# First expert's first two up-projection tiles done in token halves, and slot parts made with one operation fewer

## The chip, the cores and the metric

The kernel runs on one core of one Trainium2 chip. The metric is the device time of one execution in microseconds (us), read as the median over runs. All engine names below are those of the profile: PE is the matrix engine (PEld its weight loads), DVE the vector engine, ACT the scalar engine, POOL the engine that issues the gathers, SP the engine that issues plain transfers.

## What is computed

One layer: linear attention with a residual and a normalisation over 4096 tokens of 256 numbers, then a feed-forward block in which each of 8 experts picks its own 512 tokens. All values are float32. Cut to what matters here, the second half is

```python
logits = xf @ Wr + br                       # xf: 4096 x 256
Sm = softmax(logits, axis=-1)
G_t, idx_t = jax.lax.top_k(Sm.T, 512)       # each expert takes its 512 best tokens
tokens = xf[idx]                            # 512 rows per expert
mid = silu(einsum('keh,ehf->kef', tokens, W_up[group]) + b_up[group])   # 256 -> 682
out = einsum('kef,efh->keh', mid, W_down) + b_down                      # 682 -> 256
y = zeros_like(xf).at[idx].add(G[..., None] * out)
x = layernorm(x + y)
```

## The kernel before, in words

The program is one straight piece of code per engine; the engines meet only at semaphores, and each engine takes its instructions in the order in which they are written. The attention and the router take the first 172 us. Then the tokens of the experts are chosen, and the eight experts follow each other on PE to the end.

**Choosing tokens.** The router's probabilities lie as 128 partitions (32 token tiles x 4 experts) by 128 tokens. For experts 0 to 3 the threshold is searched in 15 rounds (lines 1075 to 1096), before any expert starts. `choose(0, ...)` (line 1098) then gives every chosen token its place in the expert's list, 1 to 512, and 0 to the others; PE turns that array (L752), and DVE splits place - 1 into the number of a list row (`part_f`, the slot divided by 4) and the column in it (`four_f`, the remainder). This takes five operations, L1128 to L1134: subtract 1 and make whole numbers, shift right, mask, and a cast of each of the two. `spread(e)` (line 1159) compares `part_f` with a constant ramp, `iotas`, and so makes 32 one-hot matrices in bfloat16 (`hot`); `lists(e)` on PE multiplies them with a small payload, which yields the token numbers of expert e (`numbers(e)` writes them to `idx`).

For experts 4 to 7 the threshold search is hidden behind the first two experts. It has ten rounds, and one round is a loop between two engines: `guess(r)` on DVE counts seven candidate thresholds, `count_second(r)` on PE adds the counts up (L757, one small matmul), `settle(r)` on DVE reads the sums (L1154) and fixes the next threshold. DVE's order around the first expert is written out by hand:

```python
numbers(1)
settle(0)      # waits for count_second(0) on PE
gates(0)
guess(1)
spread(2)
settle(1)      # waits for count_second(1) on PE
for e in range(LATE):
    expert(e)  # expert 0 begins with guess(2), settle(2), guess(3), settle(3)
```

**An expert.** POOL gathers the expert's 512 rows in four indirect transfers of 128 rows each (L1481), for expert 0 with one semaphore each. PE turns every row tile (`turn(e)`, L785, two 128x128 transposes a row tile, into banks 2 and 3 of the accumulator memory, one bank for each half of the 256 features). ACT copies both banks into `xgt` (L1378). PE multiplies `xgt` with the up weights in six feature tiles f = 0 to 5 (L798); each tile takes two matmuls of 512 columns, one for each half of the features, and every float32 matmul stands as two records in the trace. ACT applies the activation (L1383). Then follow `lists` and `turn` for later experts, and the down projection (L829), 48 records of 256 columns.

Around expert 0, PE's order before is: `lists(0)`; two 512-column filler matmuls (`warm`, L840, whose result nobody reads); `lists(1)`; `turn(0)` with a 256-column filler between its second and third row tile; `count_second(0)`; another 256-column filler; the six tiles of the up projection, with `count_second(1)` after f = 1, `count_second(2)` after f = 3 and `count_second(3)` after f = 5; then `lists(2)`, `turn(1)` and the down projection. From then on DVE makes rounds 4 to 9 of the search and the one-hot matrices of later experts while PE works.

Of the kernel before, what the change touches and what calls it, by code (L numbers as in the profile page):

```python
# [27 lines left out]
P = 128  # L28
ALU = mybir.AluOpType
# [4 lines left out]
I32 = mybir.dt.int32  # L34
# [3 lines left out]
C = D // P  # L38
# [4 lines left out]
BLK = TB * P  # L43
NT = N // P
NB = NT // TB
HALVES = BLK // 2
E = 8
GS = 2
G = E // GS
F = int(D * 4 * (2.0 / 3.0))  # L50
FT = -(-F // P)
FR = F - (FT - 1) * P
KSEL = N // E
KT = KSEL // P
# [3 lines left out]
EH = E // 2  # L58
# [42 lines left out]
def constants():  # L101
# [8 lines left out]
    c[:, C_BEFORE:C_BEFORE + P] = (p[:, None] % EH == p % EH) & (order[:, None] < order)  # L110
    c[:, C_IOTA:C_IOTA + P] = p
    c[:, C_HEAD8:C_HEAD8 + HH] = p[:, None] // HD == np.arange(HH)
# [20 lines left out]
def build(nc, x, xt, xtq, wqkv, bq, bv, wp, wpn, cols, rows, wr, wup, bup, wdn, cst, steps, out):  # L133
    with ExitStack() as ctx:
        def sb(name, shape, dt=F32):
            return ctx.enter_context(nc.sbuf_tensor(name, shape, dt))

        def sem(name):
            return ctx.enter_context(nc.semaphore(name))
# [100 lines left out]
        slot_i = sb("slot_i", [P, P], I32)  # L240
        part_i = sb("part_i", [P, P], I32)
        part_f = sb("part_f", [P, E, NT], BF16)
# [126 lines left out]
        s_gate = sem("s_gate")  # L369
        s_xtmm = sem("s_xtmm")  # L370
        s_xt = sem("s_xt")
        s_umm = sem("s_umm")
# [219 lines left out]
        def _(pe):  # L592
# [181 lines left out]
            def turn(e):  # L774

                if e:

                    pe.wait_ge(s_gat[e % 2], 16 * KT * (e // 2 + e % 2))
                for k in range(KT):
                    if e == 0:  # L780
                        if k == KT // 2:
                            warm(1, BLK // 2)
                        pe.wait_ge(s_first[k], 16)
                    for c in range(C):
                        mm = pe.transpose(ps[:, 2 + c, k * P:(k + 1) * P], xg[:, e % 2, k, c * P:(c + 1) * P], ident)  # L785
                mm.then_inc(s_xtmm, 1)

            def expert(e):
                last = e == E - 1
                pe.wait_ge(s_xt, C * e + C)  # L790
                if e % GS == 0:
                    pe.wait_ge(s_wup, 16 * (e // GS) + 16)
                for f in range(FT):
                    width = P if f < FT - 1 else FR
# [5 lines left out]
                    mm.then_inc(s_umm, 1)  # L800
                    if e == 0 and f == 1:
                        count_second(1)
                    if e < 2 and f in (3, FT - 1):
# [41 lines left out]
            lists(1)  # L845
            turn(0)
            count_second(0)
            warm(1, BLK // 2)

# [5 lines left out]
        def _(dve):  # L855
# [242 lines left out]
            def choose(h, values, level_):  # L1098
# [26 lines left out]

                done, bank, half = 5 * h, 7 if h else 0, slice(EH * h, EH * (h + 1))
                dve.wait_ge(s_pickmm, h + 1)
                dve.tensor_scalar(slot_i[:], ps[:, bank, CH:CH + P], -1.0, None, ALU.add).then_inc(s_slot, 1)  # L1128
                dve.wait_ge(s_slot, done + 1)
                dve.tensor_scalar(part_i[:], slot_i[:], KT.bit_length() - 1, None, ALU.arith_shift_right).then_inc(s_slot, 1)  # L1130
                dve.tensor_scalar(four_i[:], slot_i[:], KT - 1, None, ALU.bitwise_and).then_inc(s_slot, 1)
                dve.wait_ge(s_slot, done + 3)
                dve.tensor_copy(part_f[:, half, :], part_i[:].rearrange("p (s e) -> p e s", e=EH)).then_inc(s_slot, 1)
                dve.tensor_copy(four_f[:, half, :], four_i[:].rearrange("p (s e) -> p e s", e=EH)).then_inc(s_slot, 1)  # L1134
                dve.wait_ge(s_slot, done + 5)

# [162 lines left out]
        def _(act):  # L1299
# [91 lines left out]
            act.sem_inc(s_mid, 2)  # L1391
            turn(0)
            for e in range(LATE):
# [197 lines left out]
```

## Time and profile before

| what | value |
|---|---|
| median of 3 runs | 435.29 us (434.12 to 436.79) |
| the profiled execution, its own time | 434.87 us |
| its span in the trace | 433.1 us |
| PE busy | 368.4 us (85%) |
| DVE busy | 236.6 us (55%) |
| ACT busy | 147.7 us (34%) |
| POOL busy | 164.8 us (38%) |
| chain that ended last, by engine | PE 61%, DVE 12%, POOL 11%, DMA 5%, issue 5% |
| largest lines of that chain | L829 16%, L798 15% (both PE, the experts) |

The time of an execution is its span and some 1.8 us around it. The chain of work that ended last is followed back from the last instruction, at each step to what released it. "Granted clock" (PEclk) is the rate that TensorE was given, 1.00 for 2.4 GHz and 0.50 for 1.2 GHz. In a row of the timeline the first number is the start in us from the span's start, the second the time taken, and a bracket says how long the engine was idle before the row and what ended the idling. Rows that follow each other with the same shape are merged (x2, x8); where two kinds of rows overlap on one engine, the later starts before the earlier has ended, since the array is pipelined.

### The profile page before, as it was taken

What the parts mean: (1) busy time and instruction counts of PE and PEld (TensorE: products, weight loads), DVE (VectorE), ACT (ScalarE), POOL (GpSimd) and SP (SyncE); (2) the same over time, 40 slices, a digit from 0 to 9 for tenths busy, and PEclk for the clock granted to TensorE, in tenths of its full rate; (3) what the DMA queues carried; (4) which work ended last, traced back from release to release, by engine and by line L of the source; (5) the groups of instructions that cost most, each with busy time, mean ns of one, the idle gap of its engine ahead of it and who ended that gap; (6) DMA issues with size and microseconds to landing.
All of it is one profiled execution on the core that took longest, in us unless ns stands there. A gap on an engine that the chain in (4) does not pass through costs nothing.

```text
span 433.1 us, 5640 instructions
## 1 busy us (share of the span) xinstructions
PE 368.4 (85%) x1651; PEld 244.4 (56%) x1651; DVE 236.6 (55%) x885; ACT 147.7 (34%) x350; POOL 164.8 (38%) x250
## 2 busy tenths in 40 slices
PE   8899999899997980114899999999999999999920
PEld 7788886467775650003447565573856657374610
DVE  0775554787889888878663745513130301059450
ACT  2333323344686884330031220403112030346600
POOL 0310053001567884001703542336344243564853
PEclk9999999999999996555699999999999999999985
DMA  8935444500133554900301452416343262699641
GB/s 252 353 105 190 149 147 145 178 0 2 51 123 116 178 176 143 10 0 2 92 9 51 89 117 81 57 50 113 116 89 51 70 131 53 113 297 375 215 150 48
DMA packets 50046, 50.75 MB, mean 117 GB/s; under 512 B 12169, under 2 KB 43234, under 8 KB 50018
## 3 DMA queue, kind: packets, MB, share of 16 engines
q1 hardware_dynamic: 44066, 40.32, 31.5%
q0 software_dynamic: 5952, 10.10, 11.7%
q8 instruction: 13, 0.21, 0.2%
q14 instruction: 15, 0.12, 0.1%
HBM read 32.97 MB, written 17.43 MB: 116 GB/s over the span
## 4 chain that ended last, share of the span: by engine, by line
PE 61%; DVE 12%; POOL 11%; DMA 5%; issue 5%; SPq 3%; ACT 2%; POOLq 0%; DVEq 0%; ACTq 0%
PE ps L829 16%; PE ps L798 15%; PE ps L633 6%; PE ps L625 6%; PE ps L609 5%; PE ps L770 3%; PE ps L706 3%; POOL rstd L1435 3%; DMA heads<-ysum,idx 2%; DVE qexp L1054 2%; PE ps L719 2%; PE ps L785 1%; DMA heads<-xt 1%; POOL ysum L1488 1%; POOL xg L1481 1%
## 5 line engine op out<-in xcount | busy, mean ns | idle before, releaser
L829 PE MATMUL ps<-wdn_s,ht_all 128*128 128x256 f32 (+1 forms) x384 | 95.4, 394 | 0.0
L798 PE MATMUL ps<-xgt,wup_s 128*128 128x512 f32 (+1 forms) x192 | 87.5, 608 | 0.1
L829 PEld LDWEIGHTS ps<-wdn_s,ht_all 128*128 128x128 f32 (+1 forms) x384 | 67.8, 189 | 24.9 <-issue 18.4
L1383 ACT ACTIVATE ht_all<-ps,bup_s 128x512 f32<-128x512 f32 (+1 forms) x48 | 33.0, 687 | 122.1 <-PE ps L798 122.1
L1481 POOL DMA_INDIRECT xg<-table,idx x32 | 32.3, 1010 | 89.2 <-DVE idx L1181 46.4
L798 PEld LDWEIGHTS ps<-xgt,wup_s 128*128 128x128 f32 (+1 forms) x192 | 33.2, 182 | 47.6 <-issue 47.6
L1488 POOL DMA_INDIRECT ysum<-yb,idx x24 | 40.6, 1693 | 46.6 <-DVE yb L1213 41.1
L1213 DVE TENSOR_SCALAR yb<-ps,gate 128x256 f32<-128x256 f32 x24 | 11.6, 484 | 55.7 <-PE ps L829 55.7
L609 PE MATMUL ps<-wqkv_s,heads 128*128 128x264 f32 x128 | 33.3, 410 | 1.8 <-DMA heads<-xt 1.8
L719 PE MATMUL ps<-wp_s,turned 128*128 128x264 f32 x128 | 33.7, 385 | 0.0
L625 PE MATMUL ps<-h_all,heads 128*128 128x258 f32 (+1 forms) x128 | 30.4, 382 | 0.0
L633 PE MATMUL ps<-ht_all,wqkv_s 128*128 128x512 f32 x64 | 30.2, 594 | 0.0
L609 PEld LDWEIGHTS ps<-wqkv_s,heads 128*128 128x128 f32 x128 | 25.8, 203 | 7.0 <-issue 2.4
L625 PEld LDWEIGHTS ps<-h_all,heads 128*128 128x128 f32 x128 | 24.2, 190 | 4.1 <-DVE heads L903 0.4
L1435 POOL TENSOR_TENSOR rstd<-ve,cs 128x2 f32<-128x2 f32 (+1 forms) x34 | 25.7, 756 | 0.2
L706 PEld LDWEIGHTS ps<-kvk,qt 128*128 128x128 f32 x128 | 18.4, 190 | 11.1 <-issue 6.5
L1307 ACT ACTIVATE heads<-heads 128x512 f32<-128x512 f32 x16 | 10.1, 631 | 39.1 <-DVE heads L895 39.1
L719 PEld LDWEIGHTS ps<-wp_s,turned 128*128 128x128 f32 x128 | 21.8, 190 | 2.3
L1430 POOL TENSOR_TENSOR ve<-mv,cs 128x2 f32<-128x2 f32 (+1 forms) x34 | 8.0, 235 | 37.8 <-ACT z L1331 34.2
L706 PE MATMUL ps<-kvk,qt 128*128 128x136 f32 x128 | 19.7, 285 | 3.0 <-DVE qt L929 2.1
L1338 ACT ACTIVATE x<-us,shift,rstd 128x256 f32<-128x256 f32 x32 | 19.6, 611 | 4.3 <-POOL shift L1440 4.3
L770 PEld LDWEIGHTS ps<-pay,ht_all 128*128 128x128 bf16 x256 | 16.3, 163 | 7.7 <-DVE ht_all L1173 4.8
(193 smaller groups left out, 533.7 us busy)
## 6 DMA issues: line engine op xcount, KB each, us to landing
wdn_s<-wdn SPq DMA_DIRECT2D x8, 640.0 KB
h_all<-x SPq DMA_DIRECT2D x8, 512.0 KB, 5.6
ht_all<-xtq SPq DMA_DIRECT2D x8, 512.0 KB, 3.6
table<-x SPq DMA_DIRECT2D x32, 128.0 KB, 1.7
ysum<-x SPq DMA_DIRECT2D x32, 128.0 KB, 1.8
h_all<-ysum SPq DMA_DIRECT2D x8, 512.0 KB, 8.7
out<-h_all SPq DMA_DIRECT2D x8, 512.0 KB, 5.6
heads<-xt SPq DMA_DIRECT2D x7, 512.0 KB, 4.1
```

The source lines that it names most:

```text
L609: mm = pe.matmul(ps[:, bank + u, 0:D + E], ht_ring[:, j // 2, c, at:at + P], wqkv_s[:, c, D:W_V], start=(c == 0), stop=(c == C - 1))
L625: mm = pe.matmul(ps[:, 2 + c, 0:HC], key[:, back % 4, u, c * P:(c + 1) * P], h_all[:, bass.ds(i * 8 + (2 * back + u), 1), :].rearrange("p ...
L633: mm = pe.matmul(ps[:, m, :], wqkv_s[:, c, m * P:(m + 1) * P], ht_all[:, c, bass.ds(n * BLK, BLK)], start=(c == 0), stop=(c == C - 1))
L706: mm = pe.matmul(ps[:, 2 + t % 2, c * (P + HH):(c + 1) * (P + HH)], qt[:, c, t * P:(t + 1) * P], kvk[:, c, :], start=True, stop=True)
L719: mm = pe.matmul(bank, turned[:, (t - 1) % TB, c, :], wp_s[:, c, :], start=False, stop=(c == C - 1))
L770: mm = pe.matmul(ps[:, 6, 0:2 * KT], hot[:, :, s], pay[:, s].rearrange("p w k -> p (w k)"), start=(s == 0), stop=(s == NT - 1))
L798: mm = pe.matmul(ps[0:width, f % 2, :], wup_s[:, c, f * P:f * P + width], xgt[:, c, :], start=(c == 0), stop=(c == C - 1))
L829: mm = pe.matmul(ps[:, bank, 0:D], mid[0:rows_, f, j * P:(j + 1) * P], wdn_s[0:rows_, f, :], start=(f == 0), stop=(f == FT - 1))
L1383: act.activation(mid[0:width, f, :], ps[0:width, f % 2, :], ACT.Silu, bias=bup_s[0:width, e // GS, f:f + 1]).then_inc(s_mid, 1)
L1435: pool.tensor_tensor(rstd[:, tile, first:last], ve[:, t, first:last], cs[:, C_HALF:C_HALF + last - first], ALU.pow).then_inc(s_rs, 1)
L1481: pool.indirect_dma_start(out=xg[:, e % 2, j, :], out_offset=None, in_=table[:, :], in_offset=bass.IndirectOffsetOnAxis(ap=idx[:, e, j:j + ...
L1488: pool.indirect_dma_start(out=ysum[:, :], out_offset=bass.IndirectOffsetOnAxis(ap=idx[:, e, j:j + 1], axis=0), in_=yb[:, j, :], in_offset= ...
```

## The change

It has two parts.

**The first expert's first two tiles.** `turn(0)` is replaced by `turn_half(0)` and `turn_half(1)`, each for two of the four row tiles; half 0 goes to bank 2 and half 1 to bank 3, with both feature halves in one bank. ACT copies each half by itself (two copies of 2 x 256 elements instead of two of 512). PE's new `first_tiles()` computes f = 0 and f = 1 in four pieces of 256 tokens: f = 0 of half 0, then the turn of half 1, then f = 1 of half 0, then both tiles of half 1. Two 256-column fillers are gone. `count_second(0)`, which stood between the turn and the up projection, now stands after f = 1 of half 0; `count_second(1)` still stands after f = 1. Tiles f = 2 to 5 and everything after them are as before.

**Slot parts.** The shift and its buffer `part_i` are gone. The slot is made as place + 3 in place of place - 1, `part_f` is (place + 3) minus its remainder by 4, read from the accumulator bank again in one combined operation, so it is 4 x (row + 1), and the ramp `iotas` is scaled to match. This runs twice in the program, once for each group of four experts.

```diff
-    c[:, C_IOTA:C_IOTA + P] = p
+    c[:, C_IOTA:C_IOTA + P] = KT * (p + 1)
...
             def turn(e):
 
-                if e:
-
-                    pe.wait_ge(s_gat[e % 2], 16 * KT * (e // 2 + e % 2))
+                pe.wait_ge(s_gat[e % 2], 16 * KT * (e // 2 + e % 2))
                 for k in range(KT):
-                    if e == 0:
-                        if k == KT // 2:
-                            warm(1, BLK // 2)
-                        pe.wait_ge(s_first[k], 16)
                     for c in range(C):
                         mm = pe.transpose(ps[:, 2 + c, k * P:(k + 1) * P], xg[:, e % 2, k, c * P:(c + 1) * P], ident)
                 mm.then_inc(s_xtmm, 1)
 
+            def turn_half(half):
+
+                for k in range(2 * half, 2 * half + 2):
+                    pe.wait_ge(s_first[k], 16)
+                    for c in range(C):
+                        at = c * HALVES + k % 2 * P
+                        mm = pe.transpose(ps[:, 2 + half, at:at + P], xg[:, 0, k, c * P:(c + 1) * P], ident)
+                mm.then_inc(s_xtmm if half else s_halfmm, 1)
+
+            def up_half(f, half):
+
+                at = slice(half * HALVES, (half + 1) * HALVES)
+                for c in range(C):
+                    mm = pe.matmul(ps[:, f, at], wup_s[:, c, f * P:(f + 1) * P], xgt[:, c, at], start=(c == 0), stop=(c == C - 1))
+                return mm
+
+            def first_tiles():
+
+                pe.wait_ge(s_half, 1)
+                pe.wait_ge(s_mid, 1)
+                up_half(0, 0)
+                turn_half(1)
+                pe.wait_ge(s_mid, 2)
+                up_half(1, 0)
+                count_second(0)
+                pe.wait_ge(s_xt, C)
+                for f in range(2):
+                    up_half(f, 1).then_inc(s_umm, 1)
+                count_second(1)
+
...
-                for f in range(FT):
+                for f in range(0 if e else 2, FT):
...
-                    if e == 0 and f == 1:
-                        count_second(1)
...
-            turn(0)
-            count_second(0)
-            warm(1, BLK // 2)
+            turn_half(0)
...
-                done, bank, half = 5 * h, 7 if h else 0, slice(EH * h, EH * (h + 1))
+                done, bank, half = 4 * h, 7 if h else 0, slice(EH * h, EH * (h + 1))
+                turned_ = ps[:, bank, CH:CH + P].rearrange("p (s e) -> p e s", e=EH)
                 dve.wait_ge(s_pickmm, h + 1)
-                dve.tensor_scalar(slot_i[:], ps[:, bank, CH:CH + P], -1.0, None, ALU.add).then_inc(s_slot, 1)
+                dve.tensor_scalar(slot_i[:], ps[:, bank, CH:CH + P], KT - 1.0, None, ALU.add).then_inc(s_slot, 1)
                 dve.wait_ge(s_slot, done + 1)
-                dve.tensor_scalar(part_i[:], slot_i[:], KT.bit_length() - 1, None, ALU.arith_shift_right).then_inc(s_slot, 1)
                 dve.tensor_scalar(four_i[:], slot_i[:], KT - 1, None, ALU.bitwise_and).then_inc(s_slot, 1)
-                dve.wait_ge(s_slot, done + 3)
-                dve.tensor_copy(part_f[:, half, :], part_i[:].rearrange("p (s e) -> p e s", e=EH)).then_inc(s_slot, 1)
-                dve.tensor_copy(four_f[:, half, :], four_i[:].rearrange("p (s e) -> p e s", e=EH)).then_inc(s_slot, 1)
-                dve.wait_ge(s_slot, done + 5)
+                dve.wait_ge(s_slot, done + 2)
+                four = four_i[:].rearrange("p (s e) -> p e s", e=EH)
+                dve.scalar_tensor_tensor(out=part_f[:, half, :], in0=turned_, scalar=KT - 1.0, in1=four,
+                                         op0=ALU.add, op1=ALU.subtract).then_inc(s_slot, 1)
+                dve.tensor_copy(four_f[:, half, :], four).then_inc(s_slot, 1)
+                dve.wait_ge(s_slot, done + 4)
...
             act.sem_inc(s_mid, 2)
-            turn(0)
+            for half in range(2):
+                act.wait_ge(s_xtmm if half else s_halfmm, 1)
+                act.copy(xgt[:, :, half * HALVES:(half + 1) * HALVES],
+                         ps[:, 2 + half, :].rearrange("p (c k) -> p c k", c=C)).then_inc(s_xt if half else s_half, C if half else 1)
```

PE's order from the middle of the first expert's turn to `count_second(1)`, before. L785 is a transpose of a gathered row tile, L840 a filler, L757 a `count_second`, L798 the up projection; the bracket names the semaphores that the instruction waits for (`s_first2` is the third row tile's gather, `s_cnt2` DVE's counts, `s_xt` ACT's copies).

```order
L840 MATMUL ps<-wup_s,cs 128x256
L785 MATMUL ps<-cs,xg 128x128 [waits s_first2]
L785 MATMUL ps<-cs,xg 128x128
L785 MATMUL ps<-cs,xg 128x128 [waits s_first3]
L785 MATMUL ps<-cs,xg 128x128
L757 MATMUL ps<-cnt,same 128x7 [waits s_cnt2]
L840 MATMUL ps<-wup_s,cs 128x256
L798 MATMUL ps<-xgt,wup_s 128x512 [waits s_wup,s_mid,s_xt,s_midone]
L798 MATMUL ps<-xgt,wup_s 128x512
L798 MATMUL ps<-xgt,wup_s 128x512 [waits s_mid]
L798 MATMUL ps<-xgt,wup_s 128x512
L757 MATMUL ps<-cnt,same 128x7 [waits s_cnt2]
```

The same stretch in the changed kernel, from the first piece of the up projection to `count_second(1)`; L789 is `turn_half`, L796 `up_half`, L758 `count_second`.

```order
L796 MATMUL ps<-xgt,wup_s 128x256 [waits s_mid,s_half,s_midone]
L796 MATMUL ps<-xgt,wup_s 128x256
L789 MATMUL ps<-cs,xg 128x128 [waits s_first2]
L789 MATMUL ps<-cs,xg 128x128
L789 MATMUL ps<-cs,xg 128x128 [waits s_first3]
L789 MATMUL ps<-cs,xg 128x128
L796 MATMUL ps<-xgt,wup_s 128x256 [waits s_mid]
L796 MATMUL ps<-xgt,wup_s 128x256
L758 MATMUL ps<-cnt,same 128x7 [waits s_cnt2]
L796 MATMUL ps<-xgt,wup_s 128x256 [waits s_xt]
L796 MATMUL ps<-xgt,wup_s 128x256 x3
L758 MATMUL ps<-cnt,same 128x7 [waits s_cnt2]
```

What moved: the first `count_second` now stands behind two pieces of the up projection and the second half's transposes, and only two pieces of f = 0 and f = 1 stand between it and the next one, where there were a filler and two whole tiles. The fillers are gone.

DVE's order where the slots are split for experts 0 to 3, before, up to the first operation of `spread(0)`.

```order
L1128 TENSOR_SCALAR slot_i<-ps 128x128 [waits s_pickmm]
L1130 TENSOR_SCALAR part_i<-slot_i 128x128 [waits s_slot]
L1131 TENSOR_SCALAR four_i<-slot_i 128x128
L1133 CAST part_f<-part_i 128x128 [waits s_slot]
L1134 CAST four_f<-four_i 128x128
L1164 TENSOR_TENSOR eq<-four_f,cs 128x128 [waits s_slot,s_iotas]
```

The same place in the changed kernel.

```order
L1153 TENSOR_SCALAR slot_i<-ps 128x128 [waits s_pickmm]
L1155 TENSOR_SCALAR four_i<-slot_i 128x128 [waits s_slot]
L1158 SCALAR_TENSOR_TENSOR part_f<-ps,four_i 128x128 [waits s_slot]
L1160 CAST four_f<-four_i 128x128
L1190 TENSOR_TENSOR eq<-four_f,cs 128x128 [waits s_slot,s_iotas]
```

What moved: one operation is gone ahead of the first cast, and that cast has become a combined operation that reads the accumulator bank. DVE's order from `settle(0)` to `settle(3)` is the same in both kernels.

## Rows read from the trace of the kernel before

**Rows 1.** The chain that ended last, in order of time: start, time taken, what.

```profile
212.53 0.69 PE ps L785 x2
...
214.43 5.14 PE ps L798 x8
...
331.41 11.73 PE ps L829 x48
343.14 10.62 PE ps L798 x24
...
368.51 0.49 DVE yb L1213
```

**Rows 2.** PE in the timeline, round the first expert.

```profile
203.50 3.76 PE L840 MATMUL ps<-wup_s,cs 128*128 128x512 f32 x4
...
209.97 0.44 PE L785 MATMUL ps<-cs,xg 128*128 128x128 f32 x2 [0.27 <-DMA xg<-table,idx]
...
212.53 0.69 PE L785 MATMUL ps<-cs,xg 128*128 128x128 f32 x2 [0.65 <-DMA xg<-table,idx]
...
213.01 0.21 PE L757 MATMUL ps<-cnt,same 128*128 128x7 bf16 x1
...
219.41 0.17 PE L757 MATMUL ps<-cnt,same 128*128 128x7 bf16 x1
...
222.95 0.17 PE L757 MATMUL ps<-cnt,same 128*128 128x7 bf16 x1
...
228.69 1.07 PE L785 MATMUL ps<-cs,xg 128*128 128x128 f32 x8
```

**Rows 3.** Stretches, PE alone: length, busy us (records), granted clock, DMA share, GB/s.

```profile
210.70:217.30 6.60, 5.61 (x12) 0.50 0.38 102
217.50:222.90 5.40, 5.40 (x14) 1.00 0.00 0
302.72:306.14 3.42, 3.42 (x43) 1.00 0.60 167
```

**Rows 4.** ACT's copies: the timeline, and its line in the group by source line.

```profile
213.26 1.07 ACT L1378 COPY xgt<-ps 128x512 f32<-128x512 f32 x2 [19.37 <-PE ps L785]
...
L1378 ACT COPY xgt<-ps x16: 585/589/594, 213.3 to 380.6; 128x512 f32<-128x512 f32 x16
```

**Rows 5.** DVE in the timeline, rounds 0 to 2 of the second search.

```profile
213.29 0.17 DVE L1154 SCALAR_TENSOR_TENSOR thr<-ps,cand 128x7 f32<-128x7 f32 x1 [3.41 <-PE ps L757]
...
216.54 2.29 DVE L1173 TENSOR_TENSOR ht_all<-part_f,iotas 128x4096 bf16<-128x4096 bf16 x1
...
219.64 0.17 DVE L1154 SCALAR_TENSOR_TENSOR thr<-ps,cand 128x7 f32<-128x7 f32 x1 [0.82 <-PE ps L757]
...
222.11 0.09 DVE L1147 DVE_READ_ACCUMULATOR junk<-sv,cand 128x1 bf16 x1
...
223.19 0.17 DVE L1154 SCALAR_TENSOR_TENSOR thr<-ps,cand 128x7 f32<-128x7 f32 x1 [0.99 <-PE ps L757]
```

**Rows 6.** DVE in the timeline, the last steps of the first choice.

```profile
196.97 0.35 DVE L1119 SCALAR_TENSOR_TENSOR place<-nabove,ends,qexp 128x128 f32<-128x128 f32 x1
197.24 0.28 DVE L1122 TENSOR_TENSOR chosen<-qexp,above 128x128 f32<-128x128 f32 x1
...
198.74 0.23 DVE L1130 TENSOR_SCALAR part_i<-slot_i 128x128 int32<-128x128 int32 x1
198.88 0.22 DVE L1131 TENSOR_SCALAR four_i<-slot_i 128x128 int32<-128x128 int32 x1
199.13 0.27 DVE L1133 CAST part_f<-part_i 128x128 bf16<-128x128 int32 x1
199.32 0.27 DVE L1134 CAST four_f<-four_i 128x128 f32<-128x128 int32 x1
```

**Rows 7.** The timeline where the second group's slots are used.

```profile
276.44 2.28 DVE L1173 TENSOR_TENSOR ht_all<-part_f,iotas 128x4096 bf16<-128x4096 bf16 x1
...
281.63 2.11 PE L770 MATMUL ps<-pay,ht_all 128*128 128x8 bf16 x32
```

More of the change, by code:

```diff
@@ L240, in build @@
         slot_i = sb("slot_i", [P, P], I32)
-        part_i = sb("part_i", [P, P], I32)
         part_f = sb("part_f", [P, E, NT], BF16)
@@ L370, in build @@
         s_xtmm = sem("s_xtmm")
+        s_halfmm = sem("s_halfmm")
+        s_half = sem("s_half")
         s_xt = sem("s_xt")
@@ L786, in turn @@
                 mm.then_inc(s_xtmm, 1)
+            def turn_half(half):
[22 more added lines that the diff above has]
+                count_second(1)
             def expert(e):
                 last = e == E - 1
-                pe.wait_ge(s_xt, C * e + C)
-                if e % GS == 0:
-                    pe.wait_ge(s_wup, 16 * (e // GS) + 16)
-                for f in range(FT):
+                if e == 0:
+                    first_tiles()
+                else:
+                    pe.wait_ge(s_xt, C * e + C)
+                    if e % GS == 0:
+                        pe.wait_ge(s_wup, 16 * (e // GS) + 16)
+                for f in range(0 if e else 2, FT):
                     width = P if f < FT - 1 else FR
```

## The prediction

> **What bounds the kernel now.** I read the chain of work that ended last first. From 212.53 us on it is PE's: the transposes of the last gathered row tile, the first two up tiles, and from there one PE row after the other through all experts, until PE hands over to the last writes at 368.51 [rows 1]. So whatever starts the first expert's third tile earlier or later moves the end by as much, unless another wait takes the place. Ahead of that stretch PE waits: the timeline has it idle for the second and the fourth row tile [rows 2], and ACT's two copies stand between the last transposes and the first useful matmul, 213.22 to 214.43 [rows 1, 4]. The view of stretches says that all this runs at the lower clock: granted 0.50 (1.2 GHz) from 210.7 to 217.3, 1.00 (2.4 GHz) after that [rows 3].
>
> The second thing to see is DVE. In this stretch it is in a loop with PE, the second search. DVE idles 3.41 us until the first L757, 0.82 until the second, 0.99 until the third [rows 5]. Those idle times are the loop's slack, and it is not large.
>
> **The cost of the halves, on PE.** The first half's transposes end at 209.97 + 0.44 = 210.41 [rows 2]. ACT starts 0.04 after such an end (213.22 to 213.26) and one copy of 512 numbers a partition takes 0.59 [rows 4]; the new copy has the same 512 numbers, in two pieces. PE started 0.10 after ACT's end (214.33 to 214.43) [rows 1, 4]. So f = 0 of half 0 starts at 210.41 + 0.04 + 0.59 + 0.10 = 211.14, where before PE had its first tile at 214.43.
>
> Four records of 256 columns follow. At full clock 24 records of 512 take 10.62, 0.443 each, and 48 of 256 take 11.73, 0.244 each [rows 1]. At half clock four of 512 took 3.76, 0.94 each [rows 2]. So four of 256 cost 0.98 at full clock and between 1.77 (twice half of 0.443) and 1.88 (half of 0.94) at the lower; I take 1.8. That gives 212.94. The fourth row tile has landed by 212.53 [rows 2], so the second half's four transposes need not wait. Eight take 1.07 at full clock, and a pair 0.69 at half [rows 2]: four cost between 0.54 and 1.38, and I take 1.0, about double the full-clock price. That gives 213.94. Then f = 1 of half 0: 1.8 more at the lower clock, 0.98 if the clock has risen by then. The first count_second comes behind it, at 214.92 to 215.74. Before, it stood at 213.01 [rows 2]. So the halves bring the matmuls forward and push this one small matmul back, by 1.9 to 2.7 us. ACT's second copy (from about 214.1 to 214.8) lies beside f = 1 of half 0 and costs nothing; uncovered it would cost its 0.59 and the two hand-overs.
>
> **What is queued behind that count.** DVE's settle(0) waits for it, and behind settle(0) stand, in DVE's fixed order, gates(0), guess(1), spread(2), settle(1), guess(2). PE needs guess(2)'s counts for the third count_second, ahead of tile f = 4. DVE starts 0.28 after the count (213.01 to 213.29) and then works without a pause to the end of spread(2): 213.29 to 216.54 + 2.29 = 218.83, which is 5.54. From settle(1) to the last count of guess(2) it takes 219.64 to 222.11 + 0.09, 2.56 [rows 5]. With 0.05 to hand over to PE (ACT's was 0.04), the third count can't come sooner than 0.28 + 5.54 + 2.56 + 0.05 = 8.43 after the first. Before, the two stood 222.95 - 213.01 = 9.94 apart [rows 2], so the loop had 1.5 us to spare. A push of 1.9 to 2.7 overdraws it by 0.4 to 1.2. PE then waits twice: at the second count for guess(1), which ends 0.28 + 2.56 and a little for gates(0), some 2.9, after the first count (217.8 to 218.7), and, after two whole tiles of 3.54, some 2 us at the third count. Tile f = 4 starts 0.4 to 1.2 us later than before, although f = 2 starts earlier, by 0.7 to 1.6 (218.7 or 217.8 against 219.41).
>
> Between 0.4 and 1.2 I take 0.9, nearer to the end in which the clock stays low, since the row of this stretch has it at 0.50 throughout [rows 3]; but PE now has dense matmuls from 211.1, where before it waited for ACT, and that may raise the clock sooner. Behind the third count the search has slack again: guess(3) needs about 2.8 us and f = 4 and f = 5 take 3.5. So the 0.9 stays to the end.
>
> By the rows, sixteen records of 256 columns cost 16 x 0.244 - 8 x 0.443 = 0.36 us more than eight of 512. The Trainium skill (TensorE: Matmul & The Clock Gate, section Back-to-back issue gap) gives a matmul its columns over the clock and about 2.5 ns; counting a float32 record as two such matmuls, an estimate from that page is 0.04 us. The trace disagrees with so small a price. The forecast is the same by either, since DVE's loop sets the third count; only the gain in the first rival would be some 0.3 us larger.
>
> **The cost of the slot parts.** The chain before: L1130 at 198.74, L1131 at 198.88, the first cast at 199.13, the second at 199.32 [rows 6]. Now the mask starts where the shift did, 198.74, and takes 0.22; with the same 0.03 behind it the combined operation starts at 198.99. The trace has none that reads the accumulator bank and whole numbers in this size. The nearest one, L1119, holds DVE for 0.27 (196.97 to 197.24), the cast for 0.19 [rows 6]. So the last cast starts at 199.26, or 199.18 at the cast's price: a gain of 0.06 to 0.14; with another 0.1 for the bank it is a loss of 0.04. I take 0.06, and it moves lists(0), the gathers and all behind them. The second use, in the third expert, is hidden: its one-hot matrices end at 276.44 + 2.28 = 278.72 and PE takes them at 281.63 without a wait [rows 7].
>
> The Trainium skill (VectorE: DVE Perf Modes, section on the TRN2 errata) gives an operation that reads the accumulator memory 120 fixed cycles against 58, an estimate of 0.065 us more. By it the gain of 0.06 would be gone and the sum 0.06 higher; no row here shows it.
>
> **Sum.** 434.87 + 0.9 - 0.06 = 435.7 us against the profiled execution. That one lies 0.42 under the median of the three runs, 435.29, so I forecast 436.1 for the median.
>
> **Rivals.**
> First, a gain: the loop does not bind, and PE's earlier start carries through. It speaks for it that PE's work up to f = 2 is done 0.7 to 2.5 us sooner (two second halves from 214.92 at 0.244 a record end at 216.9; from 215.74, mostly at the lower clock, at 218.7). It decides if the first count_second comes by 214.5, that is 1.5 after its old place. Against it stands that this needs both pieces and the transposes at full clock, which no row of this stretch shows. At a gain of 1.3 and the slot's 0.06 the median would be 433.9.
>
> Second, a larger loss: PE's 2 us wait at the third count brings the clock down again behind it. In the trace the lower clock lasted from at least 210.7 to 217.3 [rows 3]; with PE busy, 6.6 us at half speed lose 3.3, half as long 1.65. That would be 437.8 to 439.4. Against it: from 302.72 to 306.14 PE had little but list matmuls and transposes, and the clock stayed at 1.00 [rows 3]. The Trainium skill (TensorE: Matmul & The Clock Gate, section HAM oscillation) warns that waits between bursts of matmuls put the clock back to half; whether 2 us between dense tiles do it, no row here shows.
>
> Third, next to nothing: the push is 1.5 to 1.7 and the slot's gain cancels it, 435.3 or so.
>
> **Chances.** Forecast 0.62, with its own range 435.4 to 437.0; first rival 0.15 (433.2 to 434.9); second 0.13; third 0.10. The range 434.2 to 438.0 holds the forecast, the third rival, and the near ends of the first two. A measurement of this kernel tells about 1% (4.4 us) from no change: under 430.9 I put 0.02, over 439.6 0.04, and 0.94 between.
>
> **What would show it.** The first count_second at 214.9 to 215.8; settle(0) 0.28 behind it; PE idle some 2 us in front of the third count, with DVE's L1147 of that kernel as the releaser; f = 4 starting at 223.4 to 224.2 instead of right behind 222.95; DVE without its idle 0.82 ahead of settle(1). I am wrong if PE does not wait at the third count, or if the granted clock is low after 224.

## The result, and the profile after

The changed kernel takes 437.33 us (median of 20 runs, 435.47 to 442.03) against 435.51 before (20 runs, 434.11 to 437.96). One run of the changed kernel, the one of 442.03, is 1.5% above its fastest, counts as slow and is left out of the ratio. The ratio is 1.0032 with a 95% interval of 1.0016 to 1.0048, so the change costs 1.4 us (0.7 to 2.1); the ratio is not the quotient of the two medians, which lie 1.82 apart. That is slower, and less than the 1% by which the chances were drawn.

| what | before | after |
|---|---|---|
| the profiled execution, its own time | 434.87 us | 436.31 us |
| its span in the trace | 433.1 us | 434.4 us |
| PE busy | 368.4 us (85%) | 366.0 us (84%) |
| DVE busy | 236.6 us (55%) | 236.0 us (54%) |
| chain that ended last: PE | 61% | 59% |
| chain that ended last: DVE | 12% | 13% |

The rows of the timeline that answer to [rows 2, 4, 5], PE, ACT and DVE round the first expert. L796 is a piece of the up projection, L789 the second half's turn, L758 `count_second`, L1180 the first operation of `settle`, L826 the whole up tiles from f = 2, L1420 ACT's copy of a half.

```profile
211.94 0.59 ACT L1420 COPY xgt<-ps 128x512 f32<-128x512 f32 x1 [16.56 <-PE ps L789]
...
212.62 2.04 PE L796 MATMUL ps<-xgt,wup_s 128*128 128x256 f32 x4 [0.72 <-issue]
...
214.46 1.06 PE L789 MATMUL ps<-cs,xg 128*128 128x128 f32 x4
...
215.31 1.23 PE L796 MATMUL ps<-xgt,wup_s 128*128 128x256 f32 x4
215.61 0.59 ACT L1420 COPY xgt<-ps 128x512 f32<-128x512 f32 x1 [3.09 <-PE ps L789]
...
216.38 0.17 PE L758 MATMUL ps<-cnt,same 128*128 128x7 bf16 x1
...
216.41 1.97 PE L796 MATMUL ps<-xgt,wup_s 128*128 128x256 f32 x8
216.59 0.17 DVE L1180 SCALAR_TENSOR_TENSOR thr<-ps,cand 128x7 f32<-128x7 f32 x1 [5.37 <-PE ps L758]
...
219.26 0.18 PE L758 MATMUL ps<-cnt,same 128*128 128x7 bf16 x1 [0.88 <-DVE junk L1173]
...
219.30 3.68 PE L826 MATMUL ps<-xgt,wup_s 128*128 128x512 f32 x8
...
219.84 2.29 DVE L1199 TENSOR_TENSOR ht_all<-part_f,iotas 128x4096 bf16<-128x4096 bf16 x1
...
222.04 0.16 DVE L1180 SCALAR_TENSOR_TENSOR thr<-ps,cand 128x7 f32<-128x7 f32 x1
...
224.65 0.18 PE L758 MATMUL ps<-cnt,same 128*128 128x7 bf16 x1 [1.67 <-DVE junk L1173]
...
224.69 3.81 PE L826 MATMUL ps<-xgt,wup_s 128*128 128x512 f32 x8
```

Up to the first count everything is where the halves should put it: f = 0 starts on half of the tokens at 212.62, and the second half's turn no longer waits for its rows. Then PE waits twice, and both times a count of DVE (L1173) ends the wait: 0.88 us at the second `count_second` and 1.67 us at the third. DVE, in turn, works from settle(0) at 216.59 to the last count of guess(2) at 224.60 without a pause in which it would wait for PE: settle(1) follows the one-hot matrices of spread(2) directly (219.84 + 2.29 = 222.13, settle(1) at 222.04), where it idled 0.82 before [rows 5].

The chain that ended last says the same. Before, it ran through PE alone in this stretch [rows 1]. Now it leaves PE at the first count and comes back at f = 4, through guess(1), spread(2) and guess(2) on DVE:

```profile
212.62 2.04 PE ps L796 x4
214.67 0.85 PE ps L789 x4
215.52 1.02 PE ps L796 x4
...
217.24 1.96 DVE junk L1173 x14
...
219.93 2.20 DVE ht_all L1199
...
222.64 1.97 DVE junk L1173 x14
...
224.83 3.66 PE ps L826 x8
```

**What two traces can be compared by.** The two spans differ by 1.3 us, but not for the reason one would read into them. PE's transpose of the places (L752 before, L753 after), ahead of anything that the change touches, stands at 197.90 before and at 199.39 after. So 1.49 us of difference are there before the first edited instruction that lies on this path. In this execution the granted clock was down for a stretch of the attention in which the code is the same in both kernels. Ahead of it PE's matmuls stand 0.20 sooner than in the execution of before, behind it 1.49 later. The stretches of the changed kernel, in the form of [rows 3], then the middle one of before, then the transpose of the places before:

```profile
69.00:72.30 3.30, 3.30 (x26) 1.00 0.48 159
72.40:75.70 3.30, 3.30 (x4) 0.50 0.50 159
75.90:80.00 4.10, 4.10 (x20) 1.00 0.72 242
```

```profile
72.40:75.70 3.30, 3.30 (x13) 1.00 0.46 159
```

```profile
197.90 0.48 PE L752 MATMUL ps<-cs,place 128*128 128x128 f32 x1 [2.17 <-DVE place L1124]
```

From here on, times in a trace are therefore given as the distance from that transpose ("behind the places"). The first down projection (the end of all that the change can touch directly in this stretch) starts at 229.60 before and at 231.30 after, 31.70 and 31.91 behind the places: in this pair the change costs 0.21 us. The rows of the chain, which start where the modelled end of the matmul ahead lies, give 0.22; before, then after:

```profile
229.76 5.77 PE ps L829 x24
```

```profile
231.47 5.77 PE ps L855 x24
```

That is less than the 1.4 us of the ratio, which is taken up with the last experiments.

The slot parts, the rows that answer to [rows 6]:

```profile
199.39 0.48 PE L753 MATMUL ps<-cs,place 128*128 128x128 f32 x1 [2.17 <-DVE place L1148]
...
200.23 0.23 DVE L1155 TENSOR_SCALAR four_i<-slot_i 128x128 int32<-128x128 int32 x1
200.49 0.37 DVE L1158 SCALAR_TENSOR_TENSOR part_f<-ps,four_i 128x128 bf16<-128x128 f32 x1
200.78 0.27 DVE L1160 CAST four_f<-four_i 128x128 f32<-128x128 int32 x1
201.20 0.29 DVE L1190 TENSOR_TENSOR eq<-four_f,cs 128x128 f32<-128x128 f32 x1 [0.15 <-DVE four_f L1160]
```

The first one-hot operation before:

```profile
199.74 0.29 DVE L1164 TENSOR_TENSOR eq<-four_f,cs 128x128 f32<-128x128 f32 x1 [0.15 <-DVE four_f L1134]
```

From the transpose of the places to the first one-hot operation it is 201.20 - 199.39 = 1.81 us, and 199.74 - 197.90 = 1.84 before: 0.03 gained. The combined operation that reads the accumulator bank holds DVE for 0.29 (200.49 to 200.78), not the 0.27 that was taken.

### The profile page after: what moved, and what is told of

Same layout as the page of the kernel before. It is cut to its first block, busy times and chain, and to the rows that moved or that the text cites. A ratio compares the mean times of both kernels' runs of the same rounds, so it can differ in the third digit from the quotient of the medians.

```text
span 434.4 us, 5646 instructions
## 1 busy us (share of the span) xinstructions
PE 366.0 (84%) x1655; PEld 243.5 (56%) x1655; DVE 236.0 (54%) x883; ACT 147.9 (34%) x350; POOL 164.5 (38%) x250
## 4 chain that ended last, share of the span: by engine, by line
PE 59%; DVE 13%; POOL 10%; DMA 6%; issue 5%; SPq 3%; ACT 1%; POOLq 0%; DVEq 0%; ACTq 0%
PE ps L855 16%; PE ps L826 13%; PE ps L634 6%; PE ps L626 6%; PE ps L610 5%; PE ps L771 3%; PE ps L707 3%; POOL rstd L1464 3%; DVE qexp L1078 2%; PE ps L720 2%; DMA out<-h_all 1%; PE ps L780 1%; DMA heads<-xt 1%; DMA heads<-ysum,idx 1%; POOL ysum L1517 1%
## 5 line engine op out<-in xcount | busy, mean ns | idle before, releaser
L826 PE MATMUL ps<-xgt,wup_s 128*128 128x512 f32 (+1 forms) x184 | 82.7, 599 | 0.0
L826 PEld LDWEIGHTS ps<-xgt,wup_s 128*128 128x128 f32 (+1 forms) x184 | 31.1, 177 | 43.9 <-issue 43.9
L610 PE MATMUL ps<-wqkv_s,heads 128*128 128x264 f32 x128 | 31.3, 389 | 3.5 <-DMA heads<-xt 3.5
L634 PE MATMUL ps<-ht_all,wqkv_s 128*128 128x512 f32 x64 | 31.9, 622 | 0.0
L610 PEld LDWEIGHTS ps<-wqkv_s,heads 128*128 128x128 f32 x128 | 24.0, 190 | 8.7 <-issue 2.8
L771 PEld LDWEIGHTS ps<-pay,ht_all 128*128 128x128 bf16 x256 | 16.3, 165 | 7.6 <-DVE ht_all L1199 4.8
```

The costliest lines, as they stand in the source:

```text
L610: mm = pe.matmul(ps[:, bank + u, 0:D + E], ht_ring[:, j // 2, c, at:at + P], wqkv_s[:, c, D:W_V], start=(c == 0), stop=(c == C - 1))
L634: mm = pe.matmul(ps[:, m, :], wqkv_s[:, c, m * P:(m + 1) * P], ht_all[:, c, bass.ds(n * BLK, BLK)], start=(c == 0), stop=(c == C - 1))
L771: mm = pe.matmul(ps[:, 6, 0:2 * KT], hot[:, :, s], pay[:, s].rearrange("p w k -> p (w k)"), start=(s == 0), stop=(s == NT - 1))
L826: mm = pe.matmul(ps[0:width, f % 2, :], wup_s[:, c, f * P:f * P + width], xgt[:, c, :], start=(c == 0), stop=(c == C - 1))
```

## The experiments

The theory is that of the prediction: the loop of count, guess and settle, entered later, sets the third count and with it f = 4. The rival is that the halves cost by themselves, with shorter matmuls, more weight loads and missing fillers. All distances below are in us behind the transpose of the places, in one trace each; ratios are to the kernel before, run beside it, with their 95% interval (as above, they are not quotients of the medians). "3rd - 1st" is the distance from the first to the third count; where PE waits at the third count it is the loop's own length.

| kernel | first count | third count | 3rd - 1st | first down projection | ratio |
|---|---|---|---|---|---|
| before | 15.11 | 25.05 | 9.94 | 31.70 | 1 |
| changed | 16.99 | 25.26 | 8.27 | 31.91 | 1.0032 (1.0016 to 1.0048) |
| slot_only | 15.02 | 24.93 | 9.91 | 31.61 | 1.0017 (0.9994 to 1.0040) |
| halves_only | 16.97 | 25.25 | 8.28 | 31.88 | 1.0050 (1.0023 to 1.0077) |
| count_late | 19.60 | 27.90 | 8.30 | 34.56 | 1.0061 (1.0036 to 1.0086) |
| count_mid | 15.94 | 24.27 | 8.34 | 30.93 | 1.0008 (0.9981 to 1.0035) |
| count_early | 12.35 | 22.35 | 10.00 | 28.96 | 0.9963 (0.9943 to 0.9983) |
| count_first | 11.53 | 22.35 | 10.82 | 28.95 | 0.9974 (0.9952 to 0.9995) |
| before_first | 11.54 | 24.75 | 13.21 | 31.44 | 0.9998 (0.9973 to 1.0024) |
| early_filler | 12.35 | 22.35 | 10.00 | 28.96 | 0.9980 (0.9954 to 1.0007) |

### Each part alone: slot_only and halves_only

`slot_only` is the kernel before with the second part of the diff (the ramp and the slot operations), `halves_only` the changed kernel with the old ramp and slot operations put back (in part):

```diff
-    c[:, C_IOTA:C_IOTA + P] = KT * (p + 1)
+    c[:, C_IOTA:C_IOTA + P] = p
...
-                dve.scalar_tensor_tensor(out=part_f[:, half, :], in0=turned_, scalar=KT - 1.0, in1=four,
-                                         op0=ALU.add, op1=ALU.subtract).then_inc(s_slot, 1)
+                dve.tensor_copy(part_f[:, half, :], part_i[:].rearrange("p (s e) -> p e s", e=EH)).then_inc(s_slot, 1)
```

> The kernel before with the slot edit alone. Theory: 0.03 us less on the path (the chain from the place's transpose to the first one-hot operation took 1.81 us in the changed kernel and 1.84 before), which no median shows: ratio 1.000 within 0.002. Rival (the combined operation that reads the accumulator bank, or the new ramp, costs something further down): the 1.4 us of the change appear here.

> The changed kernel with the old slot operations. Theory: the whole loss is in the halves, so 1 to 1.8 us above the kernel before, as the changed kernel; in the trace the distance from the first to the third count_second is 8.2 to 8.5 us and PE waits for DVE's counts at the second and third. Rival (the slot edit carries the loss): no difference from the kernel before.

The halves alone cost 2.2 us (1.0 to 3.4), not told from the change's 1.4, and their trace has the same two waits and the same 8.28 between the counts. The slot edit alone is not told from no change; its trace shows the 0.03. The loss lies in the halves.

### Only the count moved, to an earlier place: count_early

```diff
             turn_half(0)
+            count_second(0)
...
                 up_half(1, 0)
-                count_second(0)
```

> The changed kernel with one line moved: the first count_second stands right behind the first half's transposes, ahead of f = 0, and not behind f = 1 of the first half. The four pieces of the up projection stay as they are. Theory (the loop of count, guess and settle sets the third count): DVE can start settle(0) some 5 us sooner, PE's waits at the second and third count go, and the third tile starts as PE alone allows. The changed kernel waited 0.88 and 1.67 us there, so this one should be about 2 us faster than the changed kernel and 1 to 1.5 us faster than the kernel before. Rival (the halves' own price: twice as many weight loads and shorter matmuls, and the clock): the time stays that of the changed kernel, 1 to 2 us above the kernel before.

433.94 us (12 runs), 0.9963 of the kernel before: 1.6 us faster (0.7 to 2.5), and some 3 us faster than the changed kernel, by the place of one small matmul. Both are somewhat more than was expected. The theory holds and the rival falls: the four pieces, their weight loads and the missing fillers are all still there. Its timeline, PE's three counts and DVE between them:

```profile
210.01 0.17 PE L758 MATMUL ps<-cnt,same 128*128 128x7 bf16 x1
...
212.33 0.17 DVE L1216 COPY gate<-xg 128x4 f32<-128x4 f32 x1 [1.73 <-DMA xg<-table,idx]
...
215.20 2.28 DVE L1199 TENSOR_TENSOR ht_all<-part_f,iotas 128x4096 bf16<-128x4096 bf16 x1
...
216.36 0.17 PE L758 MATMUL ps<-cnt,same 128*128 128x7 bf16 x1
...
217.40 0.16 DVE L1180 SCALAR_TENSOR_TENSOR thr<-ps,cand 128x7 f32<-128x7 f32 x1
...
220.01 0.18 PE L758 MATMUL ps<-cnt,same 128*128 128x7 bf16 x1
...
220.22 0.17 DVE L1180 SCALAR_TENSOR_TENSOR thr<-ps,cand 128x7 f32<-128x7 f32 x1 [0.27 <-PE ps L758]
```

The waits at the counts are gone. DVE now waits 1.73 us for the last gathered rows in `gates(0)`, which stands ahead of guess(1), and settle(1) again starts only when spread(2) is done, 1.04 us behind the second count. The third count comes at 220.01 without a wait, but DVE idles just 0.27 ahead of settle(2), 0.21 of it from the count's start: the loop has hardly anything to spare.

### The count later, without halves: count_late

```diff
             turn(0)
-            count_second(0)
...
-                    if e == 0 and f == 1:
-                        count_second(1)
+                    if e == 0 and f < 2:
+                        count_second(f)
```

> The kernel before, no halves, no slot edit, with the first count_second moved behind the first up tile; it then stands at about 217.9 instead of 213.0, 4.9 us later. Theory: the loop had about 1.6 us to spare, so the third count comes at 217.9 + 8.3 = 226.2, 3.2 us later than before, and the time is 2.5 to 3.5 us above the kernel before, although no matmul was cut in halves. Rival (the delay of a small matmul is hidden, the halves are what costs): no difference.

438.53 us against 435.80, 2.7 us more by the ratio (1.6 to 3.7). No matmul is halved here and the fillers are in place; the third count stands 8.30 behind the first, and the waits are those of the changed kernel:

```profile
218.59 0.17 PE L757 MATMUL ps<-cnt,same 128*128 128x7 bf16 x1
...
221.50 0.18 PE L757 MATMUL ps<-cnt,same 128*128 128x7 bf16 x1 [0.91 <-DVE junk L1146]
...
226.89 0.18 PE L757 MATMUL ps<-cnt,same 128*128 128x7 bf16 x1 [1.67 <-DVE junk L1146]
```

The first count is 4.49 later than before and the first down projection 2.86: the loop's 1.64 to spare, and beyond it one for one.

### The count between the two places: count_mid

```diff
+                count_second(0)
                 pe.wait_ge(s_mid, 2)
                 up_half(1, 0)
-                count_second(0)
```

> The changed kernel with the first count_second between the second half's transposes and f = 1 of the first half, about 1.1 us sooner than in the changed kernel and 3.5 us later than in count_early. Theory: the third count stands 8.3 us behind the first, so it comes about 1 us sooner than in the changed kernel, and the time lies between the two, some 1 us below the changed kernel (ratio to the kernel before 0.999 to 1.002). Rival (count_early gained by something other than the loop, as an earlier start of f = 0): the time of count_early, ratio 0.996.

The first count comes 1.05 sooner than in the changed kernel and the first down projection 0.98 sooner; the wait at the third count is still 1.67:

```profile
215.02 0.21 PE L758 MATMUL ps<-cnt,same 128*128 128x7 bf16 x1
...
223.36 0.18 PE L758 MATMUL ps<-cnt,same 128*128 128x7 bf16 x1 [1.67 <-DVE junk L1173]
```

Its ratio, 1.0008, lies between those of the changed kernel and of count_early, as expected; by itself it is not told from either 1 or the changed kernel's. With the changed kernel and count_early this is the price of one instruction at three places: the third count comes 8.3 behind the first, until PE's own work takes longer.

### The count as early as it goes, with and without halves: count_first and before_first

```diff
                 up_half(1, 0)
-                count_second(0)
...
             lists(1)
+            count_second(0)
             turn_half(0)
...
             settle(0)
-            gates(0)
             guess(1)
             spread(2)
+            gates(0)
```

`before_first` is the same edit in the kernel before, with `turn(0)` whole; there the count is taken from behind that turn.

> The changed kernel with the first count_second ahead of the first half's transposes, and on DVE gates(0) moved from in front of guess(1) to behind spread(2), so that guess(1) no longer waits for the last gathered rows. Theory (PE, not the loop, sets the third tile once the count stands early): hardly more than count_early gave, at most 0.3 us, and 1.3 to 2 us below the kernel before; DVE idles for over 1 us ahead of settle(1). Rival (in the runs that the trace doesn't show, with a faster clock, the loop still binds in count_early): another 0.5 to 1 us.

> The kernel before, without halves and with the old slot operations, with the first count_second ahead of its turn and gates(0) behind spread(2). Theory: the loop had 1.6 us to spare there, so an earlier count buys nothing: ratio 1.000 within 0.002. Rival (the early count gains by itself, and the halves have no part in what count_early gained): 1 to 1.6 us faster than the kernel before.

count_first is not told from count_early (433.87 and 433.94 us), though DVE now has room: it idles 1.50 us ahead of settle(1) and 1.07 ahead of settle(2), and the count on PE ends both waits.

```profile
216.70 0.17 DVE L1180 SCALAR_TENSOR_TENSOR thr<-ps,cand 128x7 f32<-128x7 f32 x1 [1.50 <-PE ps L758]
...
220.32 0.17 DVE L1180 SCALAR_TENSOR_TENSOR thr<-ps,cand 128x7 f32<-128x7 f32 x1 [1.07 <-PE ps L758]
```

before_first gains nothing, 0.9998. So the early count pays only with the halves, and the halves only with the early count: before_first to count_first, which differ by the halves and the slot edit, is 31.44 to 28.95 in the traces.

### A filler put back: early_filler

Against count_early:

```diff
             turn_half(0)
             count_second(0)
+            warm(1, BLK // 2)
```

> count_early with one 256-column filler matmul behind the count, where PE waits 0.72 us for ACT's copy of the first half. Theory A (taking the two fillers out lets the clock stay low for longer in part of the runs: the halves' runs list mean granted clocks of 0.922 to 0.928 with only one in twelve at 0.932): more runs at 0.928 to 0.932, and a median 0.5 to 1.5 us below count_early. Theory B (the filler's absence does not matter): the same median within 0.2%, or up to 0.2 us more, since the filler can end 0.1 after the copy.

434.15 us, no gain over count_early's 433.94, the same places in the trace, and again one run in twelve with a mean granted clock of 0.931 or more. Theory A is not borne out: one filler put back in this place brings neither a higher clock nor time. The mean clock by itself does not say where in the span the clock was low, or whether PE had work there; what the record shows of it is taken up under what stays open.

### The same pair at other places of the clock: shifts by 1 and 2 additions

```diff
+            dve.tensor_tensor(zg[:], h_all[:, 0:TB, 0:D], h_all[:, TB:2 * TB, 0:D], ALU.add)
             choose(0, low_key, cand[:, 0:1])
```

The second shift has one such addition more, into another dead buffer.

> The kernel before with one dummy addition of 1024 numbers a partition on DVE (about 1.2 us) ahead of the first choice of tokens, so that all that follows stands some 1.2 us later against the places where the granted clock steps in the traces. It serves as the partner of after_shift1. The time itself should be 1 to 1.5 us above the kernel before.

> The changed kernel with the same dummy addition. Read against before_shift1, from the transpose of the places to the first down projection (31.70 before and 31.91 after in the unshifted pair, +0.21). Theory (what the halves cost depends on where the clock steps fall in the first expert, so one pair of traces is not the median): the pair differs by another amount here, 0.5 to 2.1 us against the change, while the distance from the first to the third count_second stays at 8.3 us and PE still waits for it. Rival (the clock has no part in it, and the medians' 1.4 us lie somewhere else in the program): +0.2 us again.

> The kernel before with two dummy additions (about 2.4 us) in the same place, the partner of after_shift2. The time should be 2 to 3 us above the kernel before.

> The changed kernel with two dummy additions. Read against before_shift2 as above. Theory: between 0.2 and 2.3 us against the change, and not the same as at the two other positions; the mean over the three positions comes nearer to the 1.4 us of the medians than the one pair does. Rival: +0.2 us at all three.

| pair | first down projection, before and changed | difference | medians | difference |
|---|---|---|---|---|
| no shift | 31.70, 31.91 | +0.21 | 435.51, 437.33 | +1.82 |
| 1 addition | 32.48, 32.96 | +0.48 | 436.58, 438.42 | +1.84 |
| 2 additions | 32.63, 31.97 | -0.66 | 438.44, 439.11 | +0.67 |

With one addition the clock did not come up at all in the first expert's gather, in either trace, and rose later: PE's stretches of before_shift1, then of after_shift1, in the form of [rows 3] (the granted clock stands behind the bracket):

```profile
208.60:212.10 3.50, 3.35 (x35) 0.50 0.20 65
212.20:220.90 8.70, 8.04 (x16) 0.50 0.33 90
221.10:226.00 4.90, 4.90 (x15) 1.00 0.00 0
```

```profile
208.60:212.10 3.50, 3.41 (x37) 0.50 0.27 75
212.20:217.60 5.40, 4.68 (x15) 0.50 0.38 100
217.80:225.00 7.20, 5.44 (x17) 1.00 0.07 19
```

Counted from the places, the changed kernel got the full clock 2.7 us sooner (18.3 against 21.0) and still reached its first down projection 0.48 later, with the same 1.67 us wait at the third count and 8.31 between the counts. With two additions the two traces fell into different patterns (the one of before into that of shift 1, with the full clock 21.4 behind the places, the changed one into that of the unshifted changed kernel, with 16.5), so that pair compares the clock and not the change. The theory of these four is borne out in that the traces' difference is not constant; it is not borne out in size. Against the kernel before, the shifts themselves cost 0.3 us (-0.8 to 1.5) for before_shift1, whose trace has the addition's 1.2 us on the path, and 2.2 (1.1 to 3.3) for before_shift2. None of the three pairs of traces shows the difference of its medians (which is itself uncertain by about 1 us where there are ten runs), so neither theory accounts for it, and the mean of the three, 0.0, is further from it than the first. The 1.4 us that the expectations call the medians' are the ratio's; the unshifted medians lie 1.82 apart.

## Why the prediction was right

The direction, the mechanism and its place were forecast as they came; the measured median, 437.33, lies in the range (434.2 to 438.0), 1.2 above the 436.1 that was named. That the number fell in the range is in part luck: see the sum.

- **The halves on PE.** f = 0 was to start 211.14 - 197.90 = 13.24 behind the places, and did at 13.23. Its four records took 1.84 (1.8 forecast), from there the second turn 0.85 (1.0) and f = 1 1.07. The last was left open between 0.98 and 1.8: the clock rose to 1.00 at some 215.7, 0.4 after it had begun at 215.31, as these rows show. That is 16.3 behind the places, where before it was 19.5 [rows 3].

```profile
210.70:212.20 1.50, 0.83 (x7) 1.00 0.41 118
212.40:215.60 3.20, 2.98 (x9) 0.50 0.40 106
215.80:222.90 7.10, 6.22 (x22) 1.00 0.14 40
```

- **The push of the first count.** 1.9 to 2.7 us were given; it was 16.99 - 15.11 = 1.88, the low end; the second turn took less than was put down, and f = 1 ran in the main at the risen clock.
- **The loop.** 8.43 us were worked out from [rows 2, 5] as the least distance between the first and the third count. It was 8.27 in the changed kernel and 8.26 to 8.34 in five others. settle(0) starts 0.21 behind the count and not 0.28, and settle(1) 0.09 before the one-hot matrices end, so the slack was 1.67 and not 1.5. The waits came where they were put: in front of the second count and, 1.67 against "some 2", in front of the third.
- **Where I chose.** Between 0.4 and 1.2 I took 0.9, nearer to the end at which the clock stays low. In the profiled execution it rose, and the third count came 0.21 later than before. This is the mis-sized term. For the trace 0.4 was the better end, less the 0.16 by which the loop was shorter. So f = 4 started at 25.30 behind the places, and not at the 25.5 to 26.3 (223.4 to 224.2) that was given as a sign.
- **The slot parts.** 0.06 forecast, 0.03 measured. The estimate from the Trainium skill (VectorE: DVE Perf Modes, section on the TRN2 errata), 0.065 us for reading the accumulator memory, would have made the gain nothing; the trace shows 0.02 more than the nearest row's 0.27, and a gain left.
- **Twice as many, shorter records.** At full clock the eight records of the second half took 1.97 us (216.41 on), 0.246 each, as the 0.244 of [rows 1] has it. An estimate from the Trainium skill (TensorE: Matmul & The Clock Gate, section Back-to-back issue gap), two of the single-matmul gaps of that section to a record, is 0.22; the trace disagrees. It made no difference, since DVE set the third count.
- **The rivals.** The gain was to come "if the first count_second comes by 214.5", 1.5 us behind its old place. count_early put it sooner than that by hand, and it came: 1.6 us against the 1.3 that the first rival was priced at. The second rival did not: after the waits the granted clock stayed at 1.00 in every trace. The row that was held against it, 302.72 to 306.14 [rows 3], could not have told: PE was busy in all of its 3.42 us, so it shows no wait. Of the third rival the trace has the size, next to nothing, but not the cause: the push was 1.88 and overdrew the slack by 0.21, and the slot's 0.03 did not cancel that.
- **The sum.** It started from the profiled execution and added 0.42 for the median. The traces bear out +0.2 for this pair and the ratio 1.4, the forecast's 0.84 lying between. Some 1 us of the measured loss is in no pair of traces, and the sum has no term for it: 0.9 was too much for the trace, and it is luck that a loss which nobody forecast brings the measurement up to it and past it.

**What stays open** is that last microsecond. It goes with the halves: in the traces count_first stands 2.5 us ahead of before_first, by the medians and ratios 1.0 to 1.3, and count_early 2.7 ahead of before, by the ratio 1.6. One rival is left that the record bears on, that the clock is low for longer in the usual run with halves than in the traced one. Each run lists its mean granted clock. Of the 96 runs of before that are listed beside the experiments 59 had 0.928 or 0.929, as the traced one (0.928); their median is 435.1 us, that of the 18 at 0.924 to 0.926 is 436.3. Of the changed kernel's 19 runs in the ratio 7 had 0.929 or more (median 436.1) and 8 had 0.925 or 0.926 (437.8), and over the six kernels with halves and no shift only 25 of 79 reached 0.928. The traces of count_early and count_first are those of the fastest of their twelve runs, at the highest clock listed (0.932 and 0.931). So lower clocks are more frequent with the halves and go with longer times, but at like clocks the changed kernel still lies 1.0 to 1.6 above before (these lists are not all from one chip). The unprofiled runs leave only a span and a mean clock, and the runs made here show neither where the clock was low in them nor why.

## What to carry to other kernels

Before moving work forward on one engine, look at every small instruction that now stands behind it, and at whose loop it starts: here one 0.2 us matmul, pushed back by 1.9 us, cost more than the halved tiles saved, and put ahead of them it turned a loss of 1.4 us into a gain of 1.6 (count_early, 433.94 us; count_first and early_filler are not told from it). The slack of such a loop can be read from one trace: the work on the other engine from entry to exit, against the distance at which the entry and exit stand now. And two traces are compared from a common instruction ahead of the edit, not by their spans.

## What the hardware showed beside this

- In all six traces with halves and no shift the granted clock rose for good 16.0 to 16.3 us behind the transpose of the places, in the four without halves 18.9 to 19.5. The earlier rise went with matmuls in the place of PE's wait for ACT (f = 0 starts 13.2 to 13.4 behind the places with halves, 16.4 to 16.5 without), wherever the first count stood. It was a side effect that the prediction left open.
- Two executions of the same instructions ahead of the edit differed by 1.49 us at the same one; over all traces of unshifted kernels that instruction stood between 197.66 and 199.54. A single trace can't carry a claim about the span of 1 us.
- The wait in front of the third count was 1.67 us in the changed kernel, halves_only, count_late, count_mid, after_shift1 and after_shift2 alike. Both ends of it hang on settle(0): DVE's guess(1), behind which the second count comes, ends 2.6 us after settle(0) starts and guess(2) 5.4 after that, while PE has some 3.7 us from the second count to the end of its two whole tiles.
